# Attention scores of two heads in one full-width matmul, in place of two half-width ones each

## What is computed

```python
q = (x @ wq).reshape(B, S, 32, 128)        # 32 query heads of 128
k = (x @ wk).reshape(B, S, 8, 128)         # 8 key/value heads, 4 query heads to each
v = (x @ wv).reshape(B, S, 8, 128)
q, k = _rope(q, pos), _rope(k, pos)
scores = einsum('bqhgd,bshd->bhgqs', q.reshape(B, S, 8, 4, 128), k) * 128 ** -0.5
scores = where(allowed, scores, neg)       # causal; the window of 256 is wider than 64 tokens
out = einsum('bhgqs,bshd->bqhgd', softmax(scores), v).reshape(B, S, 4096)
x = x + out @ wo
```

## Time and profile before

| | us |
|---|---|
| median of 3 runs | 2648.16 |
| lowest, highest | 2645.89, 2649.03 |
| the profiled execution | 2646.27 |
| its span, first to last instruction | 2644.5 |

### The profile page before, as it was taken

One profiled execution on the slowest core, in us unless ns is written; L12 is line 12 of the kernel. 1 busy time (PEld: TensorE's weight loads), 2 busy tenths in 40 slices (PEclk: granted clock), 3 DMA queues, 4 the chain that ended last, 5 costly groups with the idle time before them and its releaser, 6 DMA issues.

```text
span 2644.5 us, 35285 instructions
## 1 busy us (share of the span) xinstructions
PE 2602.4 (98%) x13448; PEld 2094.4 (79%) x13448; DVE 1338.2 (51%) x2035; ACT 833.9 (32%) x2066; POOL 1023.3 (39%) x670
## 2 busy tenths in 40 slices
PE   9999999999999999999999999999999999999999
PEld 7877777777776788888887787777777678888887
DVE  3236777777776111124623777777777511112452
ACT  2123344444444211211212334444444422121120
POOL 0034756666654533510303444333343443351030
PEclk9999999999999999999999999999999999999999
DMA  6422233333335523112543233333333451311232
GB/s 196 105 96 89 96 128 126 109 116 128 128 124 179 174 65 112 48 40 63 150 99 117 90 105 116 116 101 104 116 116 100 175 189 50 112 48 40 80 102 76
DMA packets 283065, 286.17 MB, mean 108 GB/s; under 512 B 47586, under 2 KB 225890, under 8 KB 282898
## 3 DMA queue, kind: packets, MB, share of 16 engines
q1 hardware_dynamic: 236034, 237.25, 28.6%
q10 hardware_dynamic: 46864, 46.67, 5.3%
HBM read 211.84 MB, written 72.02 MB: 107 GB/s over the span
## 4 chain that ended last, share of the span: by engine, by line
PE 90%; POOL 4%; DMA 2%; DVE 1%; SPq 1%; ACT 1%; issue 1%; POOLq 0%; ACTq 0%; DVEq 0%
PE prod L665 28%; PE prod L667 27%; PE prod L666 27%; PE turned L873 3%; PE turned L827 2%; POOL o_lo L1465 1%; POOL s_lo L1418 1%; PE turned L842 1%; PE prod L738 1%; DMA raw<-in_wo 1%; PE prod L697 1%; PE turned L857 0%; DMA raw_pair<-in_wq 0%; POOL w_lo L1398 0%; ACT probs L1188 0%
## 5 line engine op out<-in xcount | busy, mean ns | idle before, releaser
L1398 POOL TENSOR_TENSOR w_lo<-raw,w_hi 128x1024 fp32r<-128x1024 f32 x96 | 238.0, 2480 | 788.6 <-ACT w_hi L1079 788.3
L665 PE MATMUL prod<-o_hi,w_hi 128*128 128x512 f32 x1024 | 402.4, 393 | 13.6 <-POOL o_lo L1465 10.3
L667 PE MATMUL prod<-o_hi,w_lo 128*128 128x512 f32 x1024 | 398.6, 389 | 0.0
L666 PE MATMUL prod<-o_lo,w_hi 128*128 128x512 f32 x1024 | 398.6, 389 | 0.0
L1753 DVE TENSOR_TENSOR x<-prod,x 128x512 f32<-128x512 f32 x128 | 88.5, 692 | 561.7 <-PE prod L667 561.7
L1418 POOL TENSOR_TENSOR s_lo<-w_sum,s_hi 128x512 fp32r<-128x512 f32 x192 | 248.8, 1302 | 298.2 <-ACT s_hi L1156 298.2
L1079 ACT CAST w_hi<-raw 128x1024 fp32r<-128x1024 f32 x130 | 136.2, 1048 | 654.8 <-PE prod L667 527.9
L665 PE MATMUL prod<-t_hi,s_hi 128*128 128x512 f32 x768 | 311.7, 406 | 8.0 <-POOL s_lo L1418 8.0
L666 PE MATMUL prod<-t_lo,s_hi 128*128 128x512 f32 x768 | 301.0, 392 | 0.0
L667 PE MATMUL prod<-t_hi,s_lo 128*128 128x512 f32 x768 | 300.4, 391 | 0.0
L1418 POOL TENSOR_TENSOR s_lo<-raw_pair,s_hi 128x512 fp32r<-128x512 f32 x144 | 198.7, 1387 | 149.9 <-ACT s_hi L1156 146.0
(11 more groups left out here) (162 smaller groups left out, 4691.8 us busy)
## 6 DMA issues: line engine op xcount, KB each, us to landing
o_scratch<-o_out ACTq DMA_DIRECT2D x64, 512.0 KB, 3.1
raw<-in_wo SPq DMA_DIRECT2D x64, 512.0 KB, 4.1
o_raw<-o_scratch SPq DMA_DIRECT2D x64, 512.0 KB, 6.9
raw<-in_tw SPq DMA_DIRECT2D x50, 512.0 KB, 3.6
raw_pair<-in_wq SPq DMA_DIRECT2D x48, 512.0 KB, 3.8
w_sums_scratch<-w_sum SPq DMA_DIRECT2D x96, 256.0 KB, 4.4
w_sum<-w_sums_scratch SPq DMA_DIRECT2D x96, 256.0 KB, 4.5
xt_raw<-in_x SPq DMA_DIRECT2D x32, 256.0 KB, 5.7
```

Source lines behind the costliest of these rows:

```text
L665: pe.matmul(dst, wh, xh, start=start, stop=False)
L666: pe.matmul(dst, wh, xl, start=False, stop=False)
L667: return pe.matmul(dst, wl, xh, start=False, stop=stop)
L1398: pool.tensor_tensor(WL[i % 2][:], RAW[i % 2][:], WH[i % 2][:].bitcast(F32), ALU.subtract).then_inc(w_lo, 1)
```

## The change

The queries of both heads of a quad go into one buffer `Q[t]` of 1024 columns, ordered by sequence, then head, then token. A score matmul then has 128 stationary columns, the 64 queries of two heads of one sequence, against the 64 keys of that sequence, and writes all 128 partitions: 8 matmuls to a unit in place of 16. On the scores' partitions the head now stands where the sequence of a pair stood, and the probabilities, the values and the result follow: V needs no permutation (`v_cols` goes, and V is added up in 2 operations of 512 columns per group in place of 4 of 256), `pv` loops over the same 4 matmuls with other slices, and ACT's copies `p_out` and `o_out` use other views of the same sizes. No wait, semaphore or place in the order of work is changed.

```diff
-        Q = [[sb(f"q_rot{r}{t}", [P, NT], ...) for t in range(TT)] for r in range(2)]
+        Q = [sb(f"q_rot{t}", [P, 2 * NT], offset=(122 + 4 * t) * KB) for t in range(TT)]
...
-                    for b in range(BPT):
-                        for r in range(2):
-                            for s in range(2):
-                                c = b * P + s * SEQ
-                                o = (b // 2) * 2 * P + r * P + (b % 2) * SEQ
-                                mm = pe.matmul(SCB[s * SEQ:(s + 1) * SEQ, o:o + SEQ],
-                                               Q[r][t][:, c:c + SEQ], K[:, t * NT + c:t * NT + c + SEQ],
-                                               start=True, stop=True)
+                    for s in range(SPT):
+                        mm = pe.matmul(SCB[:, s * SEQ:(s + 1) * SEQ], Q[t][:, s * P:(s + 1) * P],
+                                       K[:, t * NT + s * SEQ:t * NT + (s + 1) * SEQ], start=True, stop=True)
...
-                    pt = PT[t][:].rearrange("p (m h s q) -> p m s h q", m=2, h=GQ, s=2)
-                    for s in range(2):
-                        for b in range(2):
-                            rows = slice(b * SEQ, (b + 1) * SEQ)
-                            vv = t * NT + (2 * hb + s) * HD
-                            mm = pe.matmul(view(OB[b], GQ, s * SEQ, (s + 1) * SEQ), VV[rows, vv:vv + HD],
-                                           pt[rows, hb, s], start=True, stop=True)
+                    n4 = GQ * SEQ
+                    for b in range(2):
+                        for s in range(2):
+                            rows = slice(s * SEQ, (s + 1) * SEQ)
+                            bb = 2 * hb + b
+                            mm = pe.matmul(OB[s][:, b * n4:(b + 1) * n4], VV[rows, t * NT + bb * P:t * NT + (bb + 1) * P],
+                                           PT[t][rows, bb * n4:(bb + 1) * n4], start=True, stop=True)
...
-                    act.copy(view(PT[t][:], 2, p * 2 * P, (p + 1) * 2 * P), view(TBK, 2)).then_inc(pt_in, 1)
+                    act.copy(view(PT[t][:], BPT, p * P, (p + 1) * P), view(TBK, BPT)).then_inc(pt_in, 1)
...
-                    for b in range(2):
-                        ins = act.copy(view(OS_[:], GQ, b * P, (b + 1) * P), view(OB[b], GQ))
+                    for s in range(2):
+                        ins = act.copy(OS_[:].rearrange("p (h b s n) -> p b h s n", h=GQ, b=2, s=2)[:, :, :, s],
+                                       OB[s].rearrange("p (b h n) -> p b h n", b=2, h=GQ))
...
-                    return Q[r][t][:]
+                    return view(Q[t][:], SPT, r * SEQ, (r + 1) * SEQ)
...
-                            for which, i, t in ((A_C22, PR_5, 1), (A_C21, PR_4, 0)):
-                                dve.wait_ge(qprod, q_done(n, i))
-                                for m in range(2):
-                                    xs = slice(m * 2 * P, (m + 1) * 2 * P)
-                                    ins = dve.tensor_tensor(v_cols(t, m), QB[(7 * n + i) % 4][:, xs].rearrange(
-                                        "p (b s k) -> p b s k", b=2, s=2), XU[:, xs].rearrange(
-                                        "p (b s k) -> p b s k", b=2, s=2), ALU.add)
-                                ins.then_inc(quad_in, 1)
+                            add(A_C22, VX[1][:], PR_5, XU[:])
+                            add(A_C21, VX[0][:], PR_4, XU[:])
```

More of the change, by code:

```diff
@@ L156, in build @@
         VX = [sb(f"v_rows{t}", [P, NT], offset=(116 + 2 * t) * KB) for t in range(TT)]
-        Q = [[sb(f"q_rot{r}{t}", [P, NT], offset=(122 + 4 * r + 2 * t) * KB) for t in range(TT)] for r in range(2)]
+        Q = [sb(f"q_rot{t}", [P, 2 * NT], offset=(122 + 4 * t) * KB) for t in range(TT)]
         K = sb("k_rot", [P, TOK], offset=130 * KB)
@@ L390, in fold_buf @@
             return (i + 1) % 2
-        def v_cols(t, m):
-            return VX[t][:, m * 2 * P:(m + 1) * 2 * P].rearrange("p (s b k) -> p b s k", s=2, b=2)
         def o_lo_at(hf, kb, i):
@@ L853, in turn_v @@
                     for t in range(TT):
-                        for m in range(2):
-                            for s in range(2):
-                                o = t * NT + (2 * m + s) * P
-                                mm = pe.transpose(TP[0][:, o:o + P], VX[t][:, o - t * NT:o - t * NT + P], ident)
+                        for b in range(BPT):
+                            o = t * NT + b * P
+                            mm = pe.transpose(TP[0][:, o:o + P], VX[t][:, b * P:(b + 1) * P], ident)
                     mm.then_inc(v_turned, 1)
@@ L1636, in rotate @@
                     s3 = view(src, SPT)
-                    dve.tensor_tensor(view(dst, SPT), s3, cos, ALU.mult)
+                    dve.tensor_tensor(dst, s3, cos, ALU.mult)
                     for a, b in ((0, hd2), (hd2, 0)):
@@ L1642, in rotate @@
                     dve.wait_ge(rs_in, turn)
-                    dve.tensor_tensor(dst, dst, RS[:], ALU.add).then_inc(rotated, 1)
+                    dve.tensor_tensor(dst, dst, view(RS[:], SPT), ALU.add).then_inc(rotated, 1)
                 def head_slot(gg, qd, r, t):
@@ L1649, in head_slot @@
                             dve.wait_ge(scores, 4 * (gg - 1) + 3 + t)
-                        return K[:, t * NT:(t + 1) * NT]
+                        return view(K[:, t * NT:(t + 1) * NT], SPT)
                     unit = 4 * gg + (0 if qd == QD_23 else -2) + t + 1
```

## The result

The change makes the kernel **slower by 1.1%**: the median of 5 runs is 2677.3 us (2673.3 to 2679.9) against 2647.1 for the kernel before (5 runs, 2645.9 to 2649.0), a ratio of 1.0112 (of the means) with a 95% interval of 1.0098 to 1.0127. The forecast was 2679.8. The profiled execution took 2676.9 us, 30.6 more than that of before.

What follows compares the result with a forecast made beforehand. PE alone was taken to bound the quads stages. 62 of 64 score units at 0.51 us more each give 31.6 us, everything else 0: 2648.2 + 31.6 = 2679.8 us, range 2657 to 2688 us.

Steps and rivals of the forecast that it cites:

- The bound: Middle of both quads stages: TensorE alone sets the pace, busy for all of the 470 and 460 us.
- The price of a unit: Score unit on PE: 1.28 us before, 1.79 after, read from line 697 with weight loads as the limit; 0.51 us more.
- The rival of the hidden load: Score matmuls: next weights load while columns stream, so the stream sets the pace; 22 us less, 2626 us; chance 0.08.
- that of the pace by 80 columns: Score unit: line 697's pace goes by its 80 streamed columns, so 64 cost 1.43 us; 10 us more, 2658 us; chance 0.06.
- The side-by-side loads: Score unit before: two column tiles load their 64 columns side by side, 0.060 us to a pair; the change gives this up.
- The edges: Before and behind a unit's records on PE: the change wins 0.18 us a unit, 11 us over 64 units.
- The two units that cost nothing: First unit woven into `wo` in each half: its 0.51 us only shorten a wait for POOL, so 62 of 64 units count.
- the last term of the sum: Whether a unit ending 0.51 us later starts new waits: products behind it shift equally, so taken as 0.
- The rest at nothing: V's sums (4 us less for DVE), rotations, ACT's copies, `pv`, transposes and DMAs: worth nothing to the end.
- the last rival: Strided rotation on DVE: writing runs of 64 doubles two operations; at most 88 us on top, 2768 us; chance 0.04.

Runs made afterwards that it cites:

- half_stream: The change with only the first 32 of a sequence's 64 keys streamed in each score matmul, same weight loads: 2676.9 us, ratio 1.0123 to the kernel before.
- double_stream: The change with 128 keys streamed in each score matmul (64 in the last), same weight loads: 2679.4 us, ratio 1.0132 to the kernel before.
- load96: The change with 96 in place of 128 stationary columns in each score matmul, same stream: 2650.6 us, ratio 1.0020 to the kernel before.
- tiles_in_turn: tiles_kept with all 8 score matmuls of head 0 first, then the 8 of head 1, not alternating: 2688.4 us, ratio 1.0158 to the kernel before.
- tiles_kept: The change with each score matmul split again into two of 64 stationary columns, alternating array halves: 2647.3 us, ratio 1.0008 to the kernel before.

## Why the prediction was right

**The bound.** PE alone sets the pace of the quads stages; the shares of busy time and the 470.00 of 470 said so, and the late matmuls above show that in the middle of the stages every 0.51 us on PE came out at the end.

**The price of a unit.** Forecast 1.79, measured 1.80 in the row above. That it could be read from the trace of before is luck: line 697, far away in the program, happens to have the same form but for 16 streamed columns. That these do not count was an inference from the loads' durations and from the transposes; half_stream and double_stream have shown it. The rival of the hidden load (2626 us) and that of the pace by 80 columns (2658) fall with the same two runs, and load96 excludes that the step is fixed. The steps of 0.112, 0.085 and 0.058 us for 128, 96 and 64 loaded columns lie on one line, 0.027 to 32 columns. The Trainium skill, "TensorE: Matmul & The Clock Gate", section "LDWEIGHTS", has a load take its columns / 1.2 ns, an estimated 107, 80 and 53 ns here; the runs agree, with 5 ns more each time. The Trainium skill, same page, section "Back-to-back issue gap", gives a gap by streamed columns for a matmul in isolation and says that in a stream of loads and matmuls both set the spacing; the runs agree with the second, as the step stays at 0.112 us with 32 to 128 streamed columns and falls to 0.085 with fewer loaded.

**The side-by-side loads** were the reason given for the 0.060 of a pair. tiles_in_turn shows it: with the same instructions the pair becomes two steps of 0.058. For 64 moving columns the Trainium skill, "TensorEngine Tiling (Array Packing)", section "When to Use Tiling", wants the two operands swapped as well as column tiles, which the prediction left out; both sides of a score matmul are 64 wide before the change, so no run shows what the swap is worth.

**The edges.** Forecast 0.18 us in favour of the change, from 0.32 and 0.15 to 0.23 and 0.06. Measured: 0.23 before the first record, and behind the last one (740.18 + 1.89 - 0.275 = 741.80) 0.08, so 0.16. The forecast sign shows too: ahead of the units the weight loads idled for 23.1 us in all before and for 5.5 after (groups of weight loads by line).

**The two units that cost nothing.** At the start of `wo` POOL was to absorb one unit's 0.51 us in each half. The rows of after (timeline of PE, beside the earlier trace rows):

```profile
834.44 1.90 PE L819 MATMUL turned<-k_rot,q_rot 128*128 128x64 f32 x16
836.14 0.48 PE L661 MATMUL prod<-o_hi,w_hi 128*128 128x512 f32 x1
...
838.26 0.50 PE L661 MATMUL prod<-o_hi,w_hi 128*128 128x512 f32 x1 [0.47 <-POOL o_lo L1455]
```

The product that stood at 824.27 is the third triple's first behind the unit; after, that is the one at 838.26. The first product follows the unit's start by 821.63 - 820.55 = 1.08 us before and by 836.14 - 834.44 = 1.70 after, 0.62 later; the third triple by 3.72 before and by 3.82 after, only 0.10 later. In between, 0.52 us were taken up, the unit's whole loss. The wait for POOL in the row is 0.25 shorter (0.47 in place of 0.72); the rest was gained one triple earlier, where the trace names no wait. The kernel after is 836.14 - 821.63 = 14.51 us late at the product behind the unit and 838.26 - 824.27 = 13.99 at the third triple, no more than ahead of the unit (14.00). In the second half it is the same.

**The size, 30.2 against 31.6 us.** The score matmuls lost what was forecast; what was off is the last term of the sum, other waits of PE, put at nothing. It had argued that nothing hanging on a unit runs on its own clock; three waits for POOL and DVE moved all the same. Ahead of the first product of `wo`, PE waited 0.47 us for POOL before and not at all after, and 0.40 us of the delay vanish there, 0.44 in the second half (PE, first half, before and then after):

```profile
809.26 0.47 PE L665 MATMUL prod<-o_hi,w_hi 128*128 128x512 f32 x1 [0.47 <-POOL o_lo L1465]
```

```profile
823.25 0.47 PE L661 MATMUL prod<-o_hi,w_hi 128*128 128x512 f32 x1
```

In the first group of the program a wait for a rotation before the third unit is gone (PE, before and then after):

```profile
318.18 0.60 PE L842 MATMUL turned<-consts_sb,probs 128*128 128x128 f32 x4
320.84 1.69 PE L827 MATMUL turned<-k_rot,q_rot 128*64 128x64 f32 x32 [2.06 <-DVE q_rot L1643]
```

```profile
321.72 0.60 PE L833 MATMUL turned<-consts_sb,probs 128*128 128x128 f32 x4
322.15 1.90 PE L819 MATMUL turned<-k_rot,q_rot 128*128 128x64 f32 x16
```

PE comes there 3.5 us later than before (321.72 against 318.18), the rotation's last operation on DVE only 1.2 later (it starts at 321.20 against 320.00). About half of the 3.5 us comes with the clock. The delay grows from 0.67 us ahead of the first unit to 3.00 eight products behind it; 0.51 of that is the unit's own, and the rest falls where the clock granted to TensorE is 0.50, its lower level of 1.2 GHz. Before, such a stretch came only behind the third unit, after the wait (busy time by stretch, before and then after; the clock is the third number from the end):

```profile
322.40:324.50 2.10, 2.10 (x8) 1.66 (x6) 2.05 (x4) 1.11 (x3) 2.02 (x2) 0.50 0.00 0
```

```profile
299.00:301.50 2.50, 2.50 (x7) 1.99 (x7) 2.26 (x5) 0.00 (x0) 0.47 (x1) 0.50 0.97 296
```

Both kernels had idled ahead of the first unit, for 1.40 us before and 1.48 after; why the clock fell in one of them alone is not shown. Behind the fourth unit the kernel after is thus 0.9 us late, where four units make 2.0. Little hangs on this: measured by the same sum, tiles_kept is 1.5 us early at this place and double_stream 1.5 late. Last, at the start of the second half PE waits 3.24 us for POOL's `w_lo` in place of 2.59, which adds 0.65; its cause stays open.

Together the three take off 1.3 us, about what the forecast was too high by. That it was no more is in part luck, since one of them went the other way.

**The rest at nothing** was confirmed by tiles_kept as a whole, not edit by edit. V's sums are 32 of 682 ns. The rotation's strided operations are unchanged but for chance (groups by line of after, beside the earlier trace rows: mean 871 in place of 853 ns, and 692 as before), and with that the last rival falls. The prediction had priced it too low, from 64 heads at twice 0.69 us: the rows have 128 rotations, with 0.85 us for the last operation.

```profile
L1633 DVE TENSOR_TENSOR q_rot<-q_rot,rope_sin 128x512 f32<-128x512 f32 x128 | 111.5, 871 | 4.5
L1627 DVE TENSOR_TENSOR q_rot<-prod,consts_sb 128x512 f32<-128x512 f32 x128 | 88.5, 692 | 4.4
```

## What to carry to other kernels

Before two small matmuls are joined into one of the whole array, count stationary columns and not instructions: where each matmul brings its own weights and streams few columns, the loads can set the pace, as here with up to 128 streamed columns to 128 loaded ones, and joining matmuls saves none of the loaded columns. Half-width tiles won here because they load side by side, and only while neighbouring matmuls alternated between the halves. And look for the new form elsewhere in the same trace: a line that already runs it gives the price, edges included.

## What the runs showed of the hardware beyond that

A plain fp32 matmul with 128 stationary columns takes the same step with 32, 64 or 128 streamed columns (a unit of 1.79 to 1.80 us in all three): from 32 to 128 columns, the stream cost nothing. And a half-width record that follows one in the same half takes 0.058 us, so a pair that alternates, at 0.060 by the merged rows, costs no more than one record alone.
